# Second layer norm kept as float16 halves, turned by DMA; expert-weight maxima in the shared stage

## What is computed

```python
x = x + attention(layernorm(x), context, tgt_mask, src_mask)     # + bo
xf = layernorm(x).reshape(-1, 512)
top1 = argmax(xf @ gate_w.T)                                     # which expert
masked = xf[None] * one_hot(top1).T[:, :, None]
h = relu(einsum('end,edh->enh', masked, w1) + b1[:, None, :])    # hidden 2048
expert_out = einsum('enh,ehd->end', h, w2) + b2[:, None, :]
shared = relu(xf @ sw1 + sb1) @ sw2 + sb2
x = x + expert_out.sum(axis=0) + shared
```

## Time and profile before

| | us |
|---|---|
| runs | 1948.7, 1955.52, 1953.84 |
| median | 1953.84 |
| profiled execution, its own time | 1952.96 |
| span of its profile | 1951.2 |
| TensorE busy | 1881.4 (96%) |
| TensorE weight load busy | 1197.9 (61%) |
| DVE busy | 855.0 (44%) |
| ACT busy | 849.4 (44%) |
| POOL busy | 523.9 (27%) |
| granted TensorE clock, mean | 0.99 |

### The profile page before, as it was taken

How to read it: one execution, slowest core, us unless ns; L and a number is a source line. 1 busy time by engine, 2 the same in 40 slices (tenths; PEclk the granted TensorE clock), 3 DMA queues, 4 the chain that set the end, 5 groups by cost and what they waited for, 6 DMA issues and landing times. The chain is left out here.

```text
span 1951.2 us, 35601 instructions
## 1 busy us (share of the span) xinstructions
PE 1881.4 (96%) x11964; PEld 1197.9 (61%) x11965; DVE 855.0 (44%) x1669; ACT 849.4 (44%) x1506; POOL 523.9 (27%) x635
## 2 busy tenths in 40 slices
PE   8889999999799999999999999999999999999997
PEld 6344444444466666666666666666666666666664
DVE  6988787778543333333333333222222222222222
ACT  4654444444344444444444443344443343444333
POOL 1068888888300000000000001121221111222111
PEclk9999999999899999999999999999999999999998
DMA  8245555554652222232322261611111010111100
GB/s 318 78 144 176 166 165 167 164 169 153 228 197 77 76 76 76 79 104 75 109 85 75 75 238 65 227 40 38 38 51 33 27 32 29 43 32 47 40 18 15
DMA packets 123587, 197.32 MB, mean 101 GB/s; under 512 B 20208, under 2 KB 61680, under 8 KB 123120
## 3 DMA queue, kind: packets, MB, share of 16 engines
q1 hardware_dynamic: 115584, 171.01, 26.3%
q0 software_dynamic: 7920, 25.17, 4.0%
HBM read 137.95 MB, written 58.98 MB: 101 GB/s over the span
## 5 line engine op out<-in xcount | busy, mean ns | idle before, releaser
L978 PE MATMUL pH<-room_a,room_w 128*128 128x256 f16 (+1 forms) x6336 | 768.6, 272 | 8.2 <-PEq L335 5.3
L990 PE MATMUL pY<-room_w,room_a 128*128 128x512 f16 (+1 forms) x3120 | 757.8, 380 | 4.6 <-DVE room_a L1024 4.6
L978 PEld LDWEIGHTS pH<-room_a,room_w 128*128 (+1 forms) x6336 | 612.1, 98 | 187.8 <-issue 22.0
L1024 DVE TENSOR_TENSOR room_a<-room_a 128x256 f16<-128x256 f32 (+1 forms) x528 | 233.8, 443 | 888.3 <-ACT room_a L1011 888.2
L990 PEld LDWEIGHTS pY<-room_w,room_a 128*128 128x128 f16 x3120 | 305.2, 98 | 264.5 <-DVE room_a L1024 4.9
L1009 ACT ACTIVATE room_a<-pH,e_bsel,sc 128x256 f32<-128x256 f32 (+1 forms) x272 | 151.8, 558 | 406.0 <-PE pH L978 389.7
L1009 ACT ACTIVATE room_a<-pH,b1s,sc 128x256 f32<-128x256 f32 x256 | 144.5, 565 | 365.1 <-PE pH L978 364.4
L1179 POOL TENSOR_TENSOR room_a<-room_a,s_brow 128x512 f32<-128x512 f32 x32 | 42.4, 1348 | 616.6 <-DVE room_a L1032 616.6
L461 PE MATMUL pO<-room_w,room_b 128*128 (+1 forms) x768 | 171.8, 380 | 2.7 <-DVE room_b L689 2.7
L1011 ACT ACTIVATE room_a<-pH,e_bsel,sc 128x256 f16<-128x256 f32 (+1 forms) x272 | 149.6, 550 | 0.0
L1423 POOL DMA_INDIRECT rows_room<-z_scratch,e_iz x33 | 33.7, 1021 | 415.3 <-DVE e_iz L1416 410.1
(11 more groups left out here) (184 smaller groups left out, 1546.7 us busy)
## 6 DMA issues: line engine op xcount, KB each, us to landing
room_b<-in_w SPq DMA_DIRECT2D x64, 256.0 KB, 4.5
s_er<-in_w SPq DMA_DIRECT2D x32, 512.0 KB, 6.3
room_w<-e_split SPq DMA_DIRECT2D x8, 2048.0 KB, 16.8
rows_room<-in_x SPq DMA_DIRECT2D x32, 256.0 KB, 4.6
room_a<-in_sw SPq DMA_DIRECT2D x32, 256.0 KB, 5.0
room_b<-in_x SPq DMA_DIRECT2D x32, 256.0 KB, 2.8
s_split<-room_a SPq DMA_DIRECT2D x64, 128.0 KB, 4.2
x_scratch<-room_b SPq DMA_DIRECT2D x32, 256.0 KB, 3.1
```

The lines of the kernel that those rows point to most:

```text
L978: mm = q.matmul(self.pH[j % 2][:, 0:rows], w[:, k, j * P:(j + 1) * P], zt[:, u, k, 0:rows], start=(n == 0), stop=(n == 3 * KC - 1))
L990: mm = q.matmul(self.pY[u][r][:, :], h[:, j % self.HR, r * P:(r + 1) * P], w[:, j, :], start=(j == 0 and n == 0), stop=(j == HC - 1 and n ...
L1024: q.tensor_tensor(self.hl[:, j % self.HR, 0:rows], self.hf[:, j % self.HR, 0:rows], self.hh[:, j % self.HR, 0:rows], ALU.subtract).then_in ...
```

## The change

z is scaled by 2^11 in `rstd` (the variance is multiplied by 2^-22 before the power, for which one `tensor_tensor` becomes a `tensor_scalar`). ACT writes it twice, as float32 `zf` and as its float16 hi half; DVE subtracts (`lo_z`, L758); SP stores a row of 1024 float16, hi and lo side by side (256 KB for 128 rows, as before), to `z_split`. The x1 store and the z store are now apart in SP's order: the latter comes last in an iteration. TensorE's transposes, `hi_z` and `lo_z` of the FFN stages are gone; SP issues DMAs with `transpose=True` (L957), in the shared stage from `z_split` in DRAM, one per tile, in the expert stage from the gathered rows in SBUF, one per 128 rows. `first` waits for `z_in` of these.

`largest_w` and its loads leave attention. In the shared stage the expert weights are now loaded twice: tiles 0 to 7 take two units each (at j = 5 and 12: `idle_expert`, then two `largest`), tile 8 makes `expert_scales`, and tiles 8 to 15 split two units each. The programs of ACT, DVE, POOL and SP of the shared stage are unrolled; TensorE's stays a loop.

```diff
-                e.activation(z[:, u % 2, :], x1[:, u % 2, :], ACT.Identity, bias=shift2[:, u % 2, :],
-                             scale=rs2[:, u % 2, :]).then_inc(S["z"], 1)
+                e.activation(zf[:, u % 2, :], x1[:, u % 2, :], ACT.Identity, bias=shift2[:, u % 2, :], scale=rs2[:, u % 2, :])
+                e.activation(zs[:, u % 2, 0:DM], x1[:, u % 2, :], ACT.Identity, bias=shift2[:, u % 2, :],
+                             scale=rs2[:, u % 2, :]).then_inc(S["zh"], 1)
...
+                    e.tensor_tensor(minus_m[:, u % 2, :], mv[:, u % 2, 0:1], minus[:, :], ALU.mult)
+                    e.tensor_scalar(ve[:, u % 2, :], mv[:, u % 2, 1:2], EPS, gain ** -2, ALU.add, ALU.mult).then_inc(ves, 1)
...
+            def lo_z(e, g, u):
+                e.wait_ge(S["zh"], count(g, u))
+                e.tensor_tensor(zs[:, u % 2, DM:2 * DM], zf[:, u % 2, :], zs[:, u % 2, 0:DM], ALU.subtract).then_inc(S["z"], 1)
...
                     step(dve, g, u, -1, gate)
-                    step(dve, g, u, 2, largest_w)
                     step(dve, g, u, -1, pick)
-                    if last_tile(g, u):
-                        snet.lo_z(dve, 0, 0)
+                    step(dve, g, u, -2, lo_z)
...
-                    step(sp, g, u, -2, store)
+                    step(sp, g, u, -2, store_x1)
                     step(sp, g, u, 3, load_w)
                     step(sp, g, u, 1, store_w)
+                    step(sp, g, u, -2, store_z)
...
-    def t_z(self, q, g, u, z_count):
-        t = self.tile(g, u)
-        q.wait_ge(self.S["z_in", u], z_count * g + z_count * self.parts(g, u) // self.R)
-        at_least(q, self.S["zTl"], t)
-        for r in range(self.parts(g, u)):
-            for k in range(KC):
-                mm = q.transpose(self.pZ[:, r, k * P:(k + 1) * P], self.zb[:, u, r, k * P:(k + 1) * P], self.ident[:, :])
-        mm.then_inc(self.S["zT"], 1)
+    def transpose(self, q, t, src, r=None):
+        at_least(q, self.S["h"], HC * (t - 1))
+        dst = self.zT[:, t % self.N, :, :] if r is None else self.zT[:, t % self.N, :, r * P:(r + 1) * P]
+        q.dma_start(dst, src, transpose=True).then_inc(self.S["z_in", t % self.N], 16)
+
+    def transpose_rows(self, q, t):
+        parts = 1 if t == self.half else self.R
+        q.wait_ge(self.S["rows_in", t % self.N], 32 * (t // self.N) + 16 * parts)
+        for r in range(parts):
+            self.transpose(q, t, self.zb[:, t % self.N, r, :], r)
...
         if j == 0:
-            q.wait_ge(self.S["zTl"], self.tile(g, u) + 1)
+            q.wait_ge(self.S["z_in", u], z_count * g + z_count * self.parts(g, u) // self.R)
...
+                def load_e(q):
+                    if 2 <= q < TILES + 2:
+                        sp.wait_ge(S["seen"], 2 * (q - 1))
+                        sp.wait_ge(S["cacc"], 2 * (q - 1) + 1)
+                    if q >= TILES + 2:
+                        sp.wait_ge(S["el"], 2 * (q - TILES - 1))
+                    for i, w in enumerate((w1, w2)):
+                        sp.dma_start(er[:, q % 2, i, :, :], net.rows(units(w), q % TILES)).then_inc(S[f"e_in{q % 2}"], 16)
...
+                def largest(n, i):
+                    dve.tensor_reduce(seen[:, i, n:n + 1], er[:, n % 2, i, :, :].rearrange("p r n -> p (r n)"), AX.X, ALU.max,
+                                      apply_absolute_value=True).then_inc(S["seen"], 1)
...
-                            if j == 4 and isinstance(g, int) and g == 0 and u == 0:
+                            if j == 4 and N * g + u == PASS:
                                 expert_scales()
...
+                            for h, at in enumerate(AT):
+                                if PASS <= N * g + u < TILES and j in (at, at + 2):
+                                    split_lo(2 * (N * g + u - PASS) + h, (j - at) // 2)
+                                if 0 <= N * g + u < PASS:
+                                    if j == at:
+                                        idle_expert(2 * (N * g + u) + h)
+                                    if j in (at + 1, at + 2):
+                                        largest(2 * (N * g + u) + h, j - at - 1)
...
+                for t in range(1, SLOT_TILES):
+                    net.transpose_rows(sp, t)
```

More of the change, by code:

```diff
@@ L69, in wait_apart, with unrolled @@
         eng.wait_ge(sem, count)
+def unrolled(n, body):
+    for g in range(-1, n + 1):
+        body(g)
 def groups(eng, n, body, peel_last=1):
@@ L992, in second @@
         mm.then_inc(self.S["y"], 1)
-    def hi_z(self, q, g, u):
-        q.wait_ge(self.S["zT"], self.tile(g, u) + 1)
-        at_least(q, self.S["h"], HC * (self.tile(g, u) - 1))
-        for r in range(self.parts(g, u)):
-            v = q.activation(self.zTh[:, u, :, r * P:(r + 1) * P], self.pZ[:, r, :].rearrange("p (k n) -> p k n", k=KC), ACT.Copy,
-                             scale=LN_SCALE)
-        v.then_inc(self.S["zTh"], 1)
     def relu(self, q, g, u, j, bias):
@@ L1155, in body @@
-                def body(g):
-                    if isinstance(g, int) and g == TILES // N - 1:
-                        load_set(nc, sp, wB, e1_d, e2_d, 0, w_in)
-                    for u in range(N):
-                        if not isinstance(g, int) or g >= 0:
-                            step(sp, g, u, 2, load_z)
-                        step(sp, g, u, 1, load_r)
-                        step(sp, g, u, 1, load_e)
-                        step(sp, g, u, -1, store)
-                        step(sp, g, u, 0, store_e)
@@ L1592, in body @@
                                 step(dve, g, u, 0, pick_idle)
-                        if not first_tile(g, u, 1):
-                            step(dve, g, u, 1, net.lo_z)
                 dve.tensor_copy(flags[:, :], is0[:, :]).then_inc(S["flags"], 1)
```

248 lines of the change are left out of this document (108 added, 140 removed).

## The result

The changed kernel takes 1961.92 us (median of 5 runs, 1961.06 to 1964.72) against 1953.84 before (median of 5, 1948.7 to 1955.52). The ratio is 1.0045, with a 95% interval of 1.0032 to 1.0059: slower by 0.45%. The forecast was 1954.6 in a range of 1938 to 1977; it had 0.37 for slower by more than 0.3%. The profiled execution has a span of 1959.3, 8.1 more than before.

| stretch | before | after | difference | forecast |
|---|---|---|---|---|
| start to the second residual | 148.26 | 148.30 | 0.0 | 0 |
| 26 attention periods | 326.52 | 342.81 | +16.3 | +17.7 |
| last four periods | 41.06 | 43.79 | +2.7 | +4 |
| last residual to first FFN matmul | 5.25 | 8.61 | +3.4 | +1 |
| shared stage, tile 0 | 53.05 | 63.44 | +10.4 | +6.1 |

What follows compares the result with a forecast made beforehand. A loop of POOL and DVE instructions was taken to bound attention, TensorE both FFN stages. Losses in attention, tile 0 and boundaries against FFN gains summed to +1.65 on 1952.96: 1954.6 us, range 1938 to 1977.

Steps and rivals of the forecast that it cites:

- rs_2: Attention, POOL: a tensor_tensor becomes a tensor_scalar, 0 to 0.2 us per tile, partly in the loop, +1.
- Attention: Steady state, 26 periods: lo_z's delay of lo_x and the store wait give 13.25 us per period, +17.7 (0 to +38).
- Lo_z's hold: Attention steady state: lo_z takes the memory after norm_x for 0.45 to 0.6 us, lo_x waits, period 13.0 to 13.2.
- The second loop: Attention: the residual waits for the z store behind lo_z to land, taken as 2.6 us, period 13.2.
- Rival A: Attention: the z store lands in 3.4 us and decides the period, +38 instead of +17.7, 1975 us; chance 0.22.
- Rival B: Attention: lo_z does not delay lo_x and the store lands in 2 us, about 1933 us; chance 0.18.
- Tail: Last four attention periods: too short for the store wait, two of them lose about 2 us each, +4 (0 to 8).
- First boundary: Attention to shared stage: the last z store comes one activation and one lo_z later before the barrier, +1.
- Tile 0: Shared stage: expert load lands about 24 us behind the start, idle_expert waits, lo_h(6) about 8.2 late, +7 (0 to 9).
- Rival C: Shared stage, first tile: SP reaches the expert load earlier, so it is in time, 1947.6 us; chance 0.10.
- Second boundary: Shared stage to experts: the barrier waits for gathered rows and two transposes, +0.5 (0 to 3).
- Rival D: FFN stages: transposing DMAs take beyond 36 us per tile and bind them, over 2000 us; chance 0.05.

Runs made afterwards that it cites:

- max_only: The kernel before with only the maxima moved to the shared stage, z still float32 and turned by TensorE: 1961.74 us.
- max_fixed: max_only with tile 0's two blocks at steps 10 and 13 and the first expert set one tile later: 1955.72 us, ratio 1.0004 to the kernel before.
- relax: The changed kernel with the residual waiting for ACT's reads of x1 instead of the z store's landing: 1962.68 us.
- edges: The changed kernel with SyncE issuing transposes ahead of the last stores at both stage ends, and the first expert set one tile later: 1958.08 us.
- tile0: The changed kernel with the two blocks of the shared stage's tile 0 moved from steps 5 and 12 to 10 and 13: 1948.98 us.
- one_src_late: The changed kernel with a copy in place of lo_z's subtraction and ACT's second activation last in its iteration; computes something else: 1953.18 us.

## Why the forecast came out as it did

The mechanism was right in the large: a gain in the FFN stages at TensorE's cost of the transposes, given back in attention and in tile 0. The forecast sum was +1.65 against a measured +8.1 in the profiled spans. That it came so close is partly luck: attention with its tail and rs_2 came out 3.7 below its terms, the other stretches 10.2 above theirs, and the result, 1961.9, is at the upper edge of the forecast's own 1945 to 1962. By its terms:

1. *Attention, +17.7 forecast, +16.3 measured.* The size was right, half of the reason wrong, so part of the agreement is luck. The step that failed is "ACT gets a second activation of about 0.7, which fits into the gap before L649 may start". An activation of 0.80 pushes the evacuation 0.2 and more behind norm_x's end, so that lo_x waits 0.30 to 0.83 for ACT. Lo_z's hold, the one I named, gives 13.03 once ACT is out of the way, and ACT with hardly any hold gives 13.185. The second loop, over the store, which set the forecast's 13.25, does not decide: the store lands in 2.0, under my 2.6, and relaxing the wait leaves 13.21. The sign named for it, the z store as the residual's releaser, did not come: it is POOL's L646 in 23 of 32 tiles. Rival A, built on a landing of 3.4, is excluded by the same row. Rival B (the loop is untouched) is excluded by the period of 13.185 itself. That DVE is relieved is worth nothing that can be told from scatter: with three DVE instructions fewer the period is 12.48 in max_only and 12.56 in max_fixed.
2. *rs_2, +1 forecast.* POOL's first instruction of the pair to its last takes 325.71 to 326.87 = 1.16 after, and 1.04 before (317.71 to 318.75): 0.12 per period, inside the 0.63. Within the bounds.
3. *Tail, +4 against +2.7*: right in size; of the 2.7, relax takes back 1.4, so the store loop is about half of it, and the rest stays open.
4. *First boundary, +1 against +3.4.* The step that failed is that the boundary was counted as one activation and one lo_z more, without SyncE's order: the weights of the first step stand behind a z store of two tiles back, which itself waits for lo_z, and behind 4.45 us of issuing two transposes. That this order is the cause is read from the trace; the run that changed the order, edges, moved other waits with it.
5. *Tile 0, +7 against +11.3* (the 10.4 and the 0.87 that left it). The wait itself was foreseen with its place; the failed step is "it lands about 24 behind the start". I had let SyncE reach the load several us earlier for one z load less ahead of it. It did not: in max_only, where that z load is still there, the weights land at 28.6, and here at 28.4. The rows of before added up plainly, 539.34 − 521.09 + 9.1, give 27.4. Of the 11.3 us, 8.27 is TensorE's idle time and about 2.5 the two groups of matmuls at a granted clock of 0.50. The price of 7 was taken from tile 1 of before, whose window 583 to 589 us has a granted clock of 0.50 as well, so the lower clock was in it unnamed. Rival C (in time) is excluded; tile0 shows the cause.
6. *Shared tiles, −12.2 against −9.9.* The 12 tiles 2 to 13 give 0.87 each, as forecast; tile 1, in which DVE's slots() is the limit, gives 0.50. Missing beside that are 1.9 in tile 14, where I said that the new blocks cost nothing: the lengths of DVE's and ACT's blocks were hidden, but a store that SyncE issues late, behind the blocked set, and for which ACT's next split waits, was not in the reckoning.
7. *Second boundary, −0.6 against +0.4.* The wait for the gathered rows and their two transposes costs about 1 more than the +0.5 I gave it. Moving these transposes ahead of the last store (edges) takes 2.2 off.
8. *Experts, −15.4 against −15.2*: 1.08 per tile where 0.87 + 0.2 was forecast. Rival D is excluded: 4.3 us for a transposed 512 KB against the 4.0 of a plain load.

Of the Trainium skill's two statements on transposing DMAs, "Advanced Engine Details and Errata", section "X-Bar Transpose (TRN2)" (as fast as regular ones), agrees with 4.3 against 4.0; the 1309 ns per block of "VectorE: DVE Perf Modes", section "The three transpose paths", would give an estimated 21 us for sixteen blocks in a row, and no such time shows here.

What stays open: the period of 12.77 in one_src_late is still 0.21 above that of before. The rows offer 0.12 for rs_2 and 0.19 for the copy's hold of lo_x, which together are more than that, and no run took either away alone.

## What to carry to other kernels

Where a period is a loop over two engines that take turns at the memory, look at what an added instruction holds up on the other engine in its new place: both places tried here for lo_z had a POOL instruction of the loop in them. A third engine's small delay can hide behind that cost: take the causes away one at a time and together before naming one. When a reader of a late load is moved forward, compare its new place with the load's landing time, and when DMAs are put into one queue, work out for each transfer behind them, loads and stores, when it is issued now. A change whose parts have opposite signs deserves a run for each part: here half of it was worthless and carried one 11 us stall that moving two blocks removes.

## What the runs showed of the hardware

A 512 KB float16 transpose by DMA from DRAM lands in 4.3 us (plain load 4.0), but SyncE spends 1.9 us on issuing one and 1.3 us on 128 rows from SBUF, against 0.3 to 0.5 for a plain DMA in an empty queue. A DVE float32-to-float16 copy with one source waits for a POOL tensor_tensor (1.79 us for 0.42), as an instruction with two sources does, while a reduction does not. POOL's 128x1 operations take 0.61 and 0.71 instead of 0.19 beside DVE's two-source instructions. After 8.27 us without a matmul in the shared stage TensorE went on at a granted clock of 0.50, and its next 18 matmuls took 5.1 us (573.81 to 578.9), where 18 at 1.00 take 2.65 (578.90 to 581.55).
